# A Mamba layer with mixture of experts on eight cores: the scan's input u is loaded straight into the product buffer, at each chunk's end

## The reference, cut to what matters

```python
xi = silu(conv(x @ W_in)[...])              # "u" in the kernel, 2048 channels
Bm, Cm = split(xi @ W_xproj, 2)             # 16 states each
delta = softplus(xi @ W_dt + b_dt)          # "d" in the kernel
def step(h, inp):
    u_i, d_i, B_i, C_i = inp
    dA = exp(d_i[:, None, :] * A[None, :, None])
    h = h * dA + d_i[:, None, :] * B_i[:, :, None] * u_i[:, None, :]
    y_i = sum(h * C_i[:, :, None], axis=1)
    return (h, y_i)
y = ys + xi * D_param                       # the second use of u
y = y * silu(res)
return y @ W_out
```

## Time and profile before

| what | us |
|---|---|
| median of 2 runs | 7976.36 (7966.25 to 7986.47) |
| the profiled execution: its own time | 7969.29 |
| its span (slowest core, core 7) | 7967.8 |
| spans of the 8 cores | 7896.5 to 7967.8 |
| VectorE busy | 4786.7 (60%) |
| TensorE busy | 3827.3 (48%) |
| ScalarE busy | 1403.1 (18%) |

### The profile page before, as it was taken

The page is one execution under the profiler, slowest core; times in us unless marked ns, Lnnn a source line. Parts: engine busy times, 40 slices in busy tenths (PEclk is TensorE's granted clock), DMA queues, the critical chain, the costliest instruction groups (busy, mean ns, idle before and its releaser), DMA issues.

```text
span 7967.8 us, 43746 instructions; the slowest of 8 cores (7896.5 to 7967.8 us)
## 1 busy us (share of the span) xinstructions
PE 3827.3 (48%) x16512; PEld 2035.5 (26%) x16512; DVE 4786.7 (60%) x1408; ACT 1403.1 (18%) x1270; POOL 247.3 (3%) x252
## 2 busy tenths in 40 slices
PE   3888342233233310535353353534445467676777
PEld 2776232222222210212121121211111123232232
DVE  0211067797779787979798797979863322222222
ACT  0111032332233332212112121211210000000000
POOL 0000010000000000000000000000000000000000
PEclk9987576666666655767676676767667788888888
DMA  6333787777777832020211202021021076666665
GB/s 98 116 106 104 129 122 116 100 111 113 119 100 111 117 79 42 0 58 10 48 17 41 58 0 58 10 48 26 32 69 64 22 132 121 126 117 127 116 131 101
DMA packets 468236, 640.80 MB, mean 80 GB/s; under 512 B 33886, under 2 KB 361950, under 8 KB 448046
## 3 DMA queue, kind: packets, MB, share of 16 engines
q0 software_dynamic: 380816, 352.01, 28.8%
q1 hardware_dynamic: 87214, 285.99, 15.0%
HBM read 796.49 MB, written 134.87 MB: 117 GB/s over the span
## 4 chain that ended last, share of the span: by engine, by line
DVE 55%; DMA 20%; PE 16%; another core or an unknown queue 5%; issue 2%; ACT 1%; SPq 1%; DVEq 0%; ACTq 0%; POOLq 0%; POOL 0%
DVE h_b L121 28%; DVE dBu L121 14%; DMA wr<-WrT 9%; DVE y_acc L121 8%; PE PP L994 3%; PE PP L412 2%; DMA sres_b<-sres_sp 2%; PE PP L467 2%; PE PP L427 2%; PE PP L815 1%; DMA gbc_b<-gbc_b 1%; DMA wr<-WsT 1%; DMA Cb_b<-W_dt 1%; DVE u_b L121 1%
## 5 line engine op out<-in xcount | busy, mean ns | idle before, releaser
L121 DVE TENSOR_TENSOR_SCAN h_b<-dAb,dBu 128x4112 f32<-128x4112 f32 x256 | 2233.7, 8725 | 90.8 <-ACT dBu L121 63.4
L714 PE MATMUL PP<-y_acc,sid 128*128 128x512 f32 x2048 | 1194.2, 748 | 1822.5 <-DVE y_acc L121 1822.5
L563 PE MATMUL PP<-y_acc,Cb_b 128*128 128x256 bf16 x4096 | 677.6, 338 | 1377.1 <-DMA Cb_b<-W_dt 882.7
L121 DVE TENSOR_TENSOR dBu<-du_b,Bb_b 128x4096 f32<-128x4096 f32 x256 | 1132.9, 4425 | 26.7
L714 PEld LDWEIGHTS PP<-y_acc,sid 128*128 128x128 f32 x2048 | 487.2, 245 | 2528.8 <-issue 2528.8
L121 ACT ACTIVATE dAb<-d_b,A_bc 128x4096 f32<-128x4096 f32 x256 | 951.2, 3716 | 772.3 <-DMA sres_b<-sres_sp 427.2
L994 PE MATMUL PP<-ue,wr 128*128 128x512 bf16 x4096 | 927.0, 389 | 209.1 <-DVE ue L121 113.2
L563 PEld LDWEIGHTS PP<-y_acc,Cb_b 128*128 128x128 bf16 x4096 | 485.1, 120 | 1545.8 <-issue 1405.3
L994 PEld LDWEIGHTS PP<-ue,wr 128*128 128x128 bf16 x4096 | 404.8, 100 | 732.9 <-issue 282.6
L121 DVE TENSOR_TENSOR y_acc<-h_b,Cb_b 128x4096 f32<-128x4096 f32 x128 | 566.5, 4426 | 13.7 <-DVE h_b L121 0.5
L121 ACT ACTIVATE carry<-h_b 128x16 f32<-128x16 f32 x256 | 59.2, 231 | 2762.4 <-DVE h_b L121 2762.4
(11 more groups left out here) (104 smaller groups left out, 1999.0 us busy)
## 6 DMA issues: line engine op xcount, KB each, us to landing
Cb_b<-W_dt POOLq DMA_DIRECT2D x128, 1024.0 KB, 12.0
wr<-WrT POOLq DMA_DIRECT2D x64, 2048.0 KB, 14.8
u_sp<-u_b SPq DMA_DIRECT2D x20, 2048.0 KB, 6.8
u_b<-u_sp SPq DMA_DIRECT2D x20, 2048.0 KB, 18.2
d_sp<-sres_b POOLq DMA_DIRECT2D x16, 2048.0 KB, 11.8
d_b<-d_sp SPq DMA_DIRECT2D x16, 2048.0 KB, 12.6
Bb_b<-bc_hbm SPq DMA_DIRECT2D x16, 2048.0 KB, 45.7
xib_sp<-xib_b SPq DMA_DIRECT2D x16, 1024.0 KB, 7.6
```

Source lines behind the costliest of these rows:

```text
L121: inst = fn(*a, **k)
L563: cT.inc(te.matmul(pb[bb][:, 0:TA], slab[:, kt * 256 + i * 128: kt * 256 + (i + 1) * 128], xib2[:, kt * TA:(kt + 1) * TA], start=(kt == 0) ...
L714: cT.inc(te.matmul(PP[:, zb * 512:(zb + 1) * 512], sid128[:], y_acc[:, zb * 512:(zb + 1) * 512], start=(n == 0), stop=(n == NST - 1)), 1 i ...
```

## The change

`u_b` is no longer read by the product d * u. That product now reads u from `du_b`, into which u is loaded, and writes its result over it in place. `u_b` is left for the product u * D of chunks 8 to 15 alone.

```diff
@@ before the loop
         rB.dma(syE, out=d_b[:], in_=d_sp[0])
-        rB.dma(syE, out=u_b[:], in_=u_sp[0])
+        rB.dma(syE, out=du_b[:], in_=u_sp[0])
         bchain(syE, Bb_b, 0, 0)
@@ the start of a chunk
             ve.wait_ge(*ev_cur)
-            cV.inc(ve.tensor_mul(du_b[:], d_b[:], u_b[:]))
+            cV.inc(ve.tensor_mul(du_b[:], d_b[:], du_b[:]))
             dumult_V = cV.n
@@ the loop over the states
-                if n == 1 and ch + 1 < NCH and not real:
-                    syE.wait_ge(cV.sem, dumult_V)
-                    rB.dma(syE, out=u_b[:], in_=u_sp[ch + 1])
                 if n == NST - 1:
                     dufree_V = cV.n
                     if ch + 1 < NCH:
@@
                         rB.dma(syE, out=d_b[:], in_=d_sp[ch + 1])
                         syE.wait_ge(cV.sem, dufree_V)
+                        rB.dma(syE, out=du_b[:], in_=u_sp[ch + 1])
                         bchain(syE, Bb_b, 0, ch + 1)
@@ the end of chunk 7
                 if ch + 1 == NRE:
                     syE.wait_ge(cL.sem, a2st['spill'])
                     rB.dma(syE, out=sres_b[:], in_=sres_sp[NRE])
+                    rB.dma(syE, out=u_b[:], in_=u_sp[NRE])
```

## The result

The changed kernel takes 8162.25 us in the median of 11 runs (8131.66 to 8213.96), against 7988.13 us (10 runs) for the kernel before: a ratio of 1.0223 (95% interval 1.0192 to 1.0254). The measured time lies above the forecast range of 8034 to 8124. The profiled execution took 8168.38 us, its span 8166.8.

The account below looks back on a forecast made before the run. VectorE was taken as saturated inside chunks and waiting on SP's DMA queue at chunk ends; 16 added loads cost 43.4 + 12.4 + 34.0 = 89.8 us, giving 8059.1, plus 7.1 to the median: 8066 us, range 8034 to 8124.

Parts of the forecast that it names:

- The ends of the chunks are chains of DMAs: Phase B: VectorE is saturated inside chunks (209.4 us); 15 chunk-end waits, 595.4 us, end with SP's last DMA.
- The three edits that cost nothing: Phase B: in-place d * u, the retargeted load before chunk 0, and removed early loads in chunks 0 to 7 change nothing.
- 6.2 us for each load in the first half: Ends of chunks 0 to 6: each added `du_b` load costs 6.2 us beside POOL's slabs, 43.4 in all.
- After which only one scan of 8.72 us is left.: Chunk ends: `du_b` waits for the last multiply by B, leaving one 8.72 us scan, during which `Bb_b` was already loading.
- 4.85 us for each load at the ends of chunks 8 to 14: Ends of chunks 8 to 14, no slabs: each added load costs the low price of 4.85 us, 34.0 in all.
- The high price of 9.25: Chunk ends: upper price per added load, 4.85 us plus 4.4 for another core's traffic; all 16 give 148 us.
- End of chunk 7: 12.4: End of chunk 7: two added loads, `du_b` and `u_b`, in a similar crowd, cost 2 x 6.2 = 12.4 us.
- `Bb_b` takes 59.2 us in one place and 47.2 in another for the same 2 MB, and I take that as given.: Chunk ends: the broadcast load's differing lengths, 59.2 and 47.2 us, were taken as given.
- 358 GB/s by core when both stream, 94 us in all: Chunk ends: by the skill's shared-memory rate, 2.1 MB takes an estimated 5.9 us, 16 loads 94 us.
- The hidden load: Chunk ends: the added load hides beside `Bb_b` and costs nothing, 7976 us; chance 0.07.
- the give-back: Chunks 0 to 6: removing early loads that slowed the slabs returns up to 55 us, 8011 in all; chance 0.04.
- The whole latency: Chunk ends: `Bb_b` only starts once `du_b` has landed, 12.2 us a load, 195 in all, 8172 us; chance 0.05.

Follow-up runs that it names:

- run 1: Changed kernel with chunks 8 to 15 and their loads as before, so the change acts in the first half of phase B alone; 8048.6 us, ratio 1.0066 to before.
- runs 3 and 4: Kernel before, and changed kernel, each without the broadcast loads of B after chunk 0 and C after chunk 8; 7566.2 and 7542.4 us.
- run 4: Changed kernel without the broadcast loads of B after chunk 0 and C after chunk 8; 7542.4 us, ratio 0.9433 to before.
- run 9: Kernel before's code for chunks 8 to 15, with two extra 2 MB loads at the ends of chunks 0 to 6; 8331.1 us, ratio 1.0399 to before.
- run 2: The change at the ends of chunks 7 to 14 alone, ends of chunks 0 to 6 as before; 8139.6 us, ratio 1.0185 to before.

## Why the prediction was wrong, step by step

- *The ends of the chunks are chains of DMAs, and what is late there is what VectorE waits for; the bodies do not move.* Right: the rise of the waits at the 15 ends makes up 185.5 of the 201 us between the two executions, on the mean of the cores.
- *The three edits that cost nothing.* Right for the body: no new stall, and run 1 shows no gain or loss beyond its 7 loads.
- *6.2 us for each load in the first half.* Right: 6.5 between the slowest cores, 6.9 on the mean.
- *"After which only one scan of 8.72 us is left."* True of the first half alone. In chunks 8 to 14 VectorE works on for 36 us after `Bb_b` is issued (3443.91 to 3480.3). The forecast did not hang on it, as it had `Cb_b`, `u_b` and the gate behind.
- *4.85 us for each load at the ends of chunks 8 to 14, "where most of the neighbours' loads are in step with ours".* This is the step that failed: it measured 17.0 on the mean. The neighbours are not in step there: in before's own trace they are 36.2 us apart on the mean. About half of the 17.0, 8.5 us, is the distance of the pair that is no longer reached: 36.2 - 27.2 = 9 us at 0.94 us each. The other 8 to 8.5 stands at equal distance: 4.85 of the load's own, and some 3.5 that I put down to the broadcasts that run at half speed for longer. The landings of `Bb_b` agree (8.2 us later on the first core of a pair and 15.4 on the second), but no run isolates this part. The high price of 9.25 had about this second part; it left the first out.
- *End of chunk 7: 12.4.* It was 18.5 on the mean, 9.2 a load, the high price.
- *"`Bb_b` takes 59.2 us in one place and 47.2 in another for the same 2 MB, and I take that as given."* What lies behind that difference, how much of the load falls together with the neighbour's, was the cause. I had named a drift of the neighbours' loads as what would make the forecast wrong, and gave it no price, though before's own trace shows it: on core 7, the second of its pair, the wait falls from 41.6 to 27.1 over 7 equal ends.
- *358 GB/s by core when both stream, 94 us in all (the Trainium skill, "HBM Reference", "Specifications (TRN2)").* In size it fits the 4.85 to 6.2 us of a plain load. The broadcast of `Bb_b` is far under that figure in both of its states, 89 GB/s and 45, so an estimate from it says nothing of what an added load does to a broadcast.
- *The rivals.* The hidden load and the give-back did not come. The whole latency came near in time (8172), which is chance: the broadcast moves as soon as `du_b`'s bytes have (the rows under runs 3 and 4), and run 4 has the same added loads and costs next to nothing.

Open is what sets the distance of a pair. From the start of chunk 8 to that of chunk 15 it grows by 12 us on the mean in the kernel before (30.5 to 42.6), by 7 in the changed one (26.1 to 32.7), and by 24 in run 9 (from 7.7). Some 4 of the 9 us between the two kernels are already there at the start of chunk 8, and so they are in run 2, where the ends of chunks 0 to 6 are those of before. A run that sets the distance by itself was not tried: all cores run one program. Open too is what limits the broadcasts at their two rates.

## What to carry to other kernels

Before pricing a transfer that is added at a point where all cores wait for memory, look at the same transfer on several cores and at several times; if one size takes 29 us here and 59 there, the spread is the mechanism, and an added load can move the kernel along it. A change that only renames a buffer, so that two uses no longer collide, gains nothing while one wait still stands for all loads, and here it costs 2%. The same edit with a semaphore for each use was 1.8% faster than before; what the split alone would have given was not measured. And of a buffer that is read piece by piece, each piece can be loaded again as soon as its last reader is done (5.6% faster with the change and split waits, 5.0% in the kernel before).

## What was not expected of the hardware

- One plain load of 2 MB on the other core of the pair slows a broadcast load to about one half while it lasts (89 to 48 GB/s).
- Two cores that collide at such points drift apart by themselves, from 6 to 11 us to 31 or 32 in 7 ends (run 9), and wait less the further apart they are: 61.6 us an end at 7 us of distance in run 9, 29.4 at 42 in the kernel before, with the same code there.
- While `Bb_b` was loading at 46 GB/s on core 7 of the kernel before, nothing on POOL's queue moved: from 1279 to 1300 only SP's queue has packets, though POOL had issued the store to `d_sp` at 1278.1 and two loads of W_dt at 1278.7. The store landed 43.0 us after its issue; the median of these stores is 11.8. What held it is not shown.
